# Loading the rows of a two-stage mixing and convolution kernel by channel, in a new order of SyncE's queue

## What is computed

```python
W = weights[condition]                       # one 128x128 matrix for each sequence
x = x + einsum('bct,bcd->bdt', x, W)
K = 2 * einsum('hn,hnl->hl', Ct, exp(P)).real    # one kernel of 2048 taps for each channel
y = causal_convolution(x, K) + x * D         # the reference does it by FFT of length 4096
x = x + y * (arange(2048) < length)          # beyond its length a sequence keeps x
```

## Time and profile before

| | |
|---|---|
| median of 3 runs | 1151.96 us (1150.91 to 1155.68) |
| the profiled execution: its own time | 1153.82 us |
| its span, first to last instruction | 1151.9 us |
| TensorE busy | 1013.1 us, 88% of the span |
| VectorE, ScalarE, GpSimd busy | 53%, 48%, 39% |
| mean granted TensorE clock | 0.985 |
| moved by DMA | 304.06 MB |

### The profile page before, as it was taken

The page is one execution under the profiler, slowest core; times in us unless marked ns, Lnnn a source line. Parts: engine busy times, 40 slices in busy tenths (PEclk is TensorE's granted clock), DMA queues, the critical chain, the costliest instruction groups (busy, mean ns, idle before and its releaser), DMA issues.

```text
span 1151.9 us, 28340 instructions
## 1 busy us (share of the span) xinstructions
PE 1013.1 (88%) x9478; PEld 744.9 (65%) x9478; DVE 614.1 (53%) x1518; ACT 547.5 (48%) x1163; POOL 445.5 (39%) x542
## 2 busy tenths in 40 slices
PE   6977788777738988999999999999999999999997
PEld 2332243222227777788787788787788788778876
DVE  6989800000015655566666566656656666566654
ACT  2644344344324545555455455555455555545543
POOL 2211223000105445545544544554544554554520
PEclk9999999999979999999999999999999999999999
DMA  9999999999995889898988988889999898998884
GB/s 331 421 423 423 424 422 380 423 424 424 423 337 138 208 191 208 199 225 207 205 211 221 204 214 216 204 206 228 201 211 216 202 210 215 214 208 215 209 206 111
DMA packets 219125, 304.06 MB, mean 264 GB/s; under 512 B 78850, under 2 KB 177538, under 8 KB 210898
## 3 DMA queue, kind: packets, MB, share of 16 engines
q1 hardware_dynamic: 218402, 302.37, 90.7%
q10 hardware_dynamic: 528, 1.05, 0.3%
q0 software_dynamic: 160, 0.20, 0.1%
HBM read 152.37 MB, written 134.41 MB: 249 GB/s over the span
## 4 chain that ended last, share of the span: by engine, by line
PE 43%; DMA 39%; SPq 10%; ACT 4%; issue 3%; DVE 1%; ACTq 0%; DVEq 0%
DMA u_scratch<-stage 21%; DMA u_row<-u_scratch 17%; PE bank L463 13%; PE bank L469 9%; PE bank L428 8%; PE bank L414 7%; SPq L240 5%; PE bank L402 3%; PE bank L440 3%; SPq L250 3%; ACT stage L535 3%; SPq L234 1%; DMA x_f<-in_x 1%; DVE u_t L795 0%; ACT u_t L548 0%
## 5 line engine op out<-in xcount | busy, mean ns | idle before, releaser
L463 PE MATMUL bank<-toep,u_t 128*128 128x256 f16 (+1 forms) x3072 | 396.4, 247 | 5.8 <-ACT st_sb L556 5.6
L414 PE MATMUL bank<-ident,u_row 128*128 128x128 f32 x1024 | 280.8, 279 | 49.1 <-DMA u_row<-u_scratch 43.2
L795 DVE SCALAR_TENSOR_TENSOR u_t<-bank,u_t 128x512 f16<-128x512 f32 x256 | 176.4, 689 | 265.9 <-ACT u_t L548 265.9
L469 PE MATMUL bank<-g_sb,st_sb 128*128 128x256 f16 x1536 | 306.4, 273 | 0.0
L463 PEld LDWEIGHTS bank<-toep,u_t 128*128 128x128 f16 x3072 | 282.6, 99 | 32.1 <-ACT st_sb L556 6.8
L402 PE MATMUL bank<-x_f,w_buf 128*128 128x512 f32 x512 | 240.0, 616 | 65.0 <-ACT stage L535 54.1
L556 ACT ACTIVATE st_sb<-bank 128x128 f16<-128x128 f32 x448 | 124.0, 277 | 293.3 <-PE bank L440 202.4
L800 DVE TENSOR_TENSOR st_sb<-bank,st_sb 128x128 f16<-128x128 f32 x448 | 130.7, 292 | 200.7 <-ACT st_sb L556 198.4
L402 PEld LDWEIGHTS bank<-x_f,w_buf 128*128 128x128 f32 x512 | 95.5, 195 | 205.1 <-issue 110.0
L808 DVE COPY_PREDICATED o_sb<-mask,u_row 128x512 f32<-128x512 uint8 x256 | 202.1, 789 | 16.8 <-issue 16.6
L535 ACT ACTIVATE stage<-bank 128x1024 f32<-128x1024 f32 x128 | 123.9, 1021 | 173.7 <-DMA u_scratch<-stage 151.2
(11 more groups left out here) (118 smaller groups left out, 475.8 us busy)
## 6 DMA issues: line engine op xcount, KB each, us to landing
x_f<-in_x SPq DMA_DIRECT2D x64, 1024.0 KB, 19.6
u_scratch<-stage SPq DMA_DIRECT2D x64, 1024.0 KB, 17.7
u_row<-u_scratch SPq DMA_DIRECT2D x64, 1024.0 KB, 7.6
out<-o_sb SPq DMA_DIRECT2D x256, 256.0 KB, 3.8
toep<-k_scratch SPq DMA_DIRECT2D x64, 256.0 KB, 4.8
gt_sb<-g_sb SPq DMA_TRANSPOSE x128, 4.6
nat<-in_L_cond_C SPq DMA_DIRECT2D x2, 64.0 KB, 4.9
k_scratch<-k_body POOLq DMA_DIRECT2D x4, 32.0 KB, 7.1
```

The costliest lines, as they stand in the source:

```text
L414: last = pe.transpose(bank[:, 4 + q, g * P:(g + 1) * P], u_row[c % 4][:, h, g, tb * P:(tb + 1) * P], ident[:, :])
L463: pe.matmul(bank[:, y, col + tb * P:col + Q], lhs, t[:, h, b, 0:Q - tb * P], start=first, stop=False, skip_group_check=True)
L469: last = pe.matmul(bank[:, y, col:col + Q], st[:, h, a, gr * ROWS:(gr + 1) * ROWS], g[:, h, b, :], start=False, stop=(m == 2), skip_group_ ...
L795: dve.scalar_tensor_tensor(out=t[:, q // 2, q % 2, 1, :], in0=bank[:, 4 + q, :], scalar=US, in1=t[:, q // 2, q % 2, 0, :], op0=MUL, op1=SU ...
```

## The change

The rows of a pair are loaded with one DMA for each half. Each has its own semaphore, and each waits for the two overlays that read its own half of the buffer. TensorE waits for half 0 before piece 0 and for half 1 before piece 8. In SyncE's slot the first half's load comes first, where the Toeplitz tile was; the Toeplitz tile comes after the second half's load. The transposes' semaphore is split into two, by the parity of the pair.

```diff
-        s_row = [sem(f"s_row{i}") for i in range(4)]
+        s_row = [[sem(f"s_row{i}_{h}") for h in range(2)] for i in range(4)]
...
+        s_gt = [sem(f"s_gt{i}") for i in range(2)]
...
-            def load_u(i, c):
-                wait(sp, s_ov, 4 * (UN * i + c - 3))
-                sp.dma_start(u_row[c % 4][:, :, :, :].rearrange("p h g q -> p h (g q)"),
-                             u_dram.ap()[bass.ds(2 * (UN * i + c), 2), :, :, :].rearrange("h p g q -> p h (g q)"))\
-                    .then_inc(s_row[c % 4], 16)
+            def load_u(i, c, h):
+                wait(sp, s_ov, 4 * (UN * i + c - 4) + 2 * h + 2)
+                sp.dma_start(u_row[c % 4][:, h, :, :].rearrange("p g q -> p (g q)"),
+                             bass.AP(u_dram, (2 * (UN * i + c) + h) * (ROWS * NG * Q), [[NG * Q, ROWS], [1, NG * Q]]))\
+                    .then_inc(s_row[c % 4][h], 16)
...
-                                 transpose=True).then_inc(s_gt, 16)
+                                 transpose=True).then_inc(s_gt[c % 2], 16)
...
             for c in range(2):
-                load_u(0, c)
+                for h in range(2):
+                    load_u(0, c, h)
                 load_toeplitz(0, c)
 
             def slot(i, c):
                 if has(i, c + 2):
-                    load_toeplitz(i, c + 2)
+                    load_u(i, c + 2, 0)
...
                 if has(i, c - 2):
                     store_out(i, c - 2, 1)
                 if has(i, c + 2):
-                    load_u(i, c + 2)
+                    load_u(i, c + 2, 1)
+                    load_toeplitz(i, c + 2)
                 if has(i, c - 1):
                     store_out(i, c - 1, 0)
...
-                if k == 0:
-                    pe.wait_ge(s_row[c % 4], 16 * (i + c // 4 + 1))
+                if k % 8 == 0:
+                    pe.wait_ge(s_row[c % 4][k // 8], 16 * (i + c // 4 + 1))
...
-                pe.wait_ge(s_gt, 32 * (n + 1))
+                pe.wait_ge(s_gt[c % 2], 32 * (UN // 2 * i + c // 2 + 1))
```

More of the change, by code:

```diff
@@ L153, in build @@
         s_ut, s_uh, s_ul = (sem(n) for n in ("s_ut", "s_uh", "s_ul"))
-        s_gx, s_gs, s_gh, s_g, s_go, s_lam, s_gt = (
-            sem(n) for n in ("s_gx", "s_gs", "s_gh", "s_g", "s_go", "s_lam", "s_gt"))
+        s_gx, s_gs, s_gh, s_g, s_go, s_lam = (
+            sem(n) for n in ("s_gx", "s_gs", "s_gh", "s_g", "s_go", "s_lam"))
+        s_gt = [sem(f"s_gt{i}") for i in range(2)]
         s_st, s_sth, s_stl = (sem(n) for n in ("s_st", "s_sth", "s_stl"))
```

## The result

The changed kernel takes 1113.62 us (median of 4 runs, 1111.44 to 1115.22), the kernel before 1151.43 (4 runs, 1148.86 to 1155.68): a ratio of 0.9656, with a 95% interval of 0.9628 to 0.9683. The forecast was 1116, between 1109 and 1136. The profiled execution has a span of 1113.2 us against 1151.9.

A forecast was written before the change was run, and what follows sets the result against it. The prediction took a ring of TensorE, SyncE's queue and the row load as the bound. Gains 31.4 + 5.9 + 0.8 - 1.5 = 36.6 us gave 1117.2 profiled, 1115.4 on the median; it said 1116, range 1109 to 1136.

The forecast's parts named there:

- The ring of three: Convolution slots: TensorE's end frees SyncE's queue, which issues the row load TensorE awaits; 26.2 us of waits for rows.
- Step (1): First half's load goes out about 0.5 us before the slot, wanted 11.67 us in, lands in at most 9.8: no wait.
- Step (2): Second half's load goes out near 4.6 us into the slot, wanted before piece 8 at 17.5 or later: no wait.
- Step (3): 57 convolution slots: 43 at 11.67 and 14 loop-edge ones at 12.49, 676.7 instead of 708.13 us; gain 31.4.
- Step (4): Slot 392.79 to 410.34, 17.55 us from a late load and low clock, falls to 11.67: gain 5.9.
- Step (5): Start of the stage: TensorE waits for half a load instead of a whole one; gain 0.8 us, bounds 0 and 1.6.
- Step (6): One more TensorE wait in each of 61 slots: loss 1.5 us; SyncE's extra issue hidden by 4.0 us of waiting per slot.
- Step (7): One more DMA per slot: fixed part up to 2.7 us is latency and overlaps, taken as nothing; 11.2 fits 11.87.
- A: Rival: DMA becomes the bound mildly, loads, transposes and stores stretching each other; slots of 12.15, 1131 us; chance 0.12.
- C: Rival: a second DMA costs engine time in each engine's queue, making it slower: 1168 to some 1230 us; chance 0.04.
- B: Rival: another wait, ScalarE's for a store or the state chain, replaces it every second slot; 1131 us; chance 0.07.
- D: Rival: the first half still lands late, from slow transfers ahead or SyncE late for another reason; 1150 us; chance 0.03.

The follow-up runs named there:

- the order alone: Changed kernel, but a pair's rows in one DMA again, first in SyncE's slot, waiting for all four overlays: 1114.38 us, ratio 0.9646 to the kernel before.
- the halves alone: Changed kernel, but with before's order of SyncE's slot: Toeplitz tile, transposes, second store, both half loads, first store; 1112.96 us, ratio 0.9623 to the kernel before.
- in the old place: One DMA for the rows, behind the transposes and second store as before; only the Toeplitz tile moves behind it: 1131.93 us, ratio 0.9779 to the kernel before.
- last: One DMA for the rows, last in SyncE's slot behind the first store, Toeplitz tile first as in the kernel before: 1644.33 us in one run.
- the repeat of the changed kernel: The changed kernel itself, unaltered, run once more beside later runs on the same chip: 1113.35 us, ratio 0.9632 to the kernel before.
- eight slots: Changed kernel with UN = 8, eight slots in a pass of the loop instead of four: 1151.21 us, ratio 0.9989 to the kernel before.
- straight: Changed kernel with UN = 56, the loop's body run once so that no engine jumps back: 1106.99 us, ratio 0.9579 to the kernel before.
- quarters: Changed kernel with each half's rows in two DMAs of 64 rows instead of one: 1116.96 us, ratio 0.9699 to the kernel before.
- 28: Changed kernel with UN = 28 slots in a pass, plus 90 transposes of the identity before the first rows: 1115.73 us, ratio 0.9683 to the kernel before.
- with 90: Changed kernel, four slots in a pass, plus 90 transposes of the identity on TensorE before the first rows: 1113.78 us, ratio 0.9669 to the kernel before.
- the straight code with 104: Changed kernel with UN = 56, no jump back, plus 104 transposes of the identity before the first rows: 1106.60 us, ratio 0.9572 to the kernel before.
- 104 at four slots in a pass: Changed kernel plus 104 transposes of the identity on TensorE before the first rows: 1114.81 us, ratio 0.9645 to the kernel before.

## Why the prediction was right

- **The ring of three** (TensorE's end, SyncE's queue, the load) was the bound. The chain, the waits and the placements of the load (the whole change, the order alone, the halves alone, in the old place, last) agree.
- **Step (1), first half:** forecast 0.5 us before the slot, 0.4 measured; landing at most 9.8 allowed for, 5.1 taken (median; 8.6 at most). **Step (2), second half:** 4.6 us into the slot, 5.0 measured; 5.1 to land, no wait. But neither part is needed where the other is there, which the forecast did not say. For the order it could have been read from its own numbers: a whole load behind overlay 3, 2.3 us into the slot, lands 7.6 later, at 9.9, which is below 11.67. For the halves it takes that a half lands in less than 6.2 us behind the old order (11.67 - 5.5); the median was 5.9.
- **Step (3), the slots:** 676.7 us forecast for the 57, 675.36 measured; edges 12.39 to 12.54, most of them 12.40 or 12.41, instead of the 12.49 taken, and 13 of them; the fourteenth slot, where the loop is left, takes 11.93. That the other engines would keep up showed true: TensorE waits for nothing in the ordinary slots.
- **Step (4), the long slot:** 5.9 forecast, 5.8 measured. The late load explains it, and the clock fell with the wait: before, TensorE stood from 403 to 406 at a granted clock of 1.00, and from 406 to 409, when it came back, the clock was 0.59:

```profile
403.00:406.00 3.00, 0.00 (x0) 0.00 (x0) 1.55 (x4) 1.38 (x3) 2.35 (x3) 1.00 0.97 283
406.00:409.00 3.00, 2.18 (x12) 1.81 (x13) 0.00 (x0) 0.00 (x0) 2.92 (x5) 0.59 1.22 138
```

- **Not in the sum:** slots 1 to 3 gave 1.0 us and the tail 0.3.
- **Step (5), the start, missed in this execution:** a gain of 0.8 was forecast and a loss of 0.4 came. TensorE did start sooner after its load. The chain of both executions, before and (second fence) after:

```profile
343.43 2.44 PE bank L428 x12
...
356.13 2.27 PE bank L428 x12
```

```profile
333.90 3.60 DMA u_row<-u_scratch
337.64 3.65 PE bank L417 x16
...
343.00 3.99 PE bank L431 x12
...
357.33 2.27 PE bank L431 x12
```

From the first load to the first transpose it took 3.74 instead of 5.28 us. But line 431 then ran at the lower clock (3.99 instead of 2.44 us), and that alone takes the 1.5 us back. From 343 to 347 the granted clock is 0.58 there, 1.00 before and 1.00 in the repeat of the changed kernel, whose slot 1 begins 21.6 us after the first load instead of 23.3. So the term's sign changes between executions of the same kernel. The other traces favour a gain. From the first load to slot 1 it takes 22.9, 23.5, 23.8 and 24.0 us in the four executions whose start loads whole pairs (before, order alone, last, old place), and 20.9, 21.5, 21.6, 22.4 and 23.3 us in the five that load halves and have no transposes of the identity (eight slots, straight, repeat, halves alone, the changed kernel): 1.6 us less on average, from single executions. With quarters it takes 23.2. The forecast's upper bound of 1.6 does not follow from the fixed part it points to: with the 2.7 us of (7) it is (5.15 - 2.7) / 2 = 1.2.
- **Step (6), more instructions:** 1.5 us lost in the forecast; ordinary slots take 11.68 instead of 11.67 at most, 0.6 us over 57. The cover is thinner than forecast: SyncE now stands 146.6 us in 58 waits, 2.5 us a slot instead of 3.3. The forecast took the one more issue, 0.7 us, from the 4.0, and left out that the slot itself becomes 0.6 us shorter (12.42 to 11.85).
- **Step (7), DMA:** taken as nothing, and the slots show nothing of it. But the arithmetic behind rivals A and C was wrong. It took 0.90 x 12.42 = 11.2 us as fixed DMA work of a slot. The share is 0.92 of 11.85 in the changed kernel, 0.82 with the order alone and 0.96 with quarters: 10.9, 9.7 and 11.4 us for the same bytes at nearly the same slot. So the share does not measure an amount of work. From 328 to 333 it even reads 1.51 in the changed kernel, at 207 GB/s. That a packet is booked for longer when more is in flight is the likely reason; it was not tested.
- **The Trainium skill's rule** (DMA: Bandwidth & Descriptors, Bandwidth) to batch DMAs to 1 MiB did not decide here. That page's fit, which it gives for DMAs issued from GpSimd and not from SyncE as here, makes 3.2 us for a half, an estimate; the medians measured are 5.1 in the changed kernel and 5.9 with the halves alone, single ones 3.6 to 8.6. No slot was bound by the sum of such times: the forecast's 13.2 us by that fit stand against 11.85.

No rival came. Against A and C, ordinary slots stay at 11.65 to 11.71 us, without a wait at piece 0 or 8. Against B, ScalarE never waits for a store in the 57 slots. Against D, the wait for the rows is gone.

## What to carry to other kernels

Compare the landing of a load with the length of the consumer's own work, and place it in the queue by that: once it lands inside, neither smaller pieces nor an earlier place bring more, and one of the two is enough. Read what stands ahead of it in the same queue, and what that waits for. Add to every wait of TensorE its refill, and where it is as long as the 4 to 7 us seen here, the slower work behind it. Once TensorE is the bound, look at the loop's edge, and measure a longer body before believing in it: four slots and straight code were good, eight cost the whole gain.

## What the runs showed of the hardware beyond what was expected

- The same load of 1 MB lands in 5.3 us (median) in the order in which nothing was issued for 3 us before it, in 7.6 behind two transposes and two stores, and in 7.6 right behind two stores (the load last); half of it lands in 5.1. How long a transfer takes to land says little about its size here.
- A jump back costs about 0.7 us with a body of four slots and 6 to 8 us with eight or 28. The instruction queue q8 carries 20 packets with four, 90 with eight, 82 with 28 and 77 in straight code, where TensorE hardly stands at all. With eight slots it is TensorE alone that stands at the jump, for 5.1 us on average; with four it waits 0.4 us there for ScalarE's state.
- TensorE came back at the lower of its two clock levels, 1.2 GHz, after standing for 4 to 7 us. Behind the identity's transposes it did so after standing for 1.9 us (with 90, and in the straight code with 104), and did not after 2.0 us (104 at four slots in a pass: granted clock 1.00 from 343 to 347).
